# Conditional residual layer on one core: weights of the second category behind two x tiles, bias rows in three loads, first category read from the smallest key

## The chip, the core and the metric

The kernel runs on one core of one Trainium2 chip. The metric is the device time of one execution in microseconds (us). A core has TensorE (PE in the rows; PEld is its weight load), VectorE (DVE), ScalarE (ACT), GpSimd (POOL) and SyncE (SP). SP, ACT and POOL can each put DMA transfers on a queue of their own; all queues are served by the core's 16 DMA engines.

## What is computed

```python
# x: 128 x 128 x 512, ids: 128 values of 0..30, W: 32 x 512 x 512, b: 32 x 512, all f32
selected_W = W[cat_ids]
selected_b = b[cat_ids]
y = jnp.einsum('bti,bio->bto', x, selected_W) + selected_b[:, None, :]
return x + y
```

Each of the 128 batches is a 128 x 512 tile that is multiplied by the 512 x 512 weights of its category; the category's bias row and the tile itself are added. The ids as drawn put 6 batches in category 0, 3 in category 1, 9 in category 2, 4 in category 3 and 1 to 9 in each later one up to 30.

## The kernel before

Batches are worked off sorted by category, so that each category's weights (1 MB) are loaded once. `x` is transposed on the host; tile i of the sorted order is a 256 KB load into `xs` (8 buffers). The identity is added to the weights, so that the product already holds `x` itself. A matmul of f32 precision is put together from rounded parts: ScalarE rounds a tile into its high part `xh` (L268) and copies it to PSUM (`pT`, L271), VectorE subtracts to get the low part `xl` (`low`, L329); GpSimd adds the identity to the raw weights `wr` (L224), rounds them to `wh` (L238) and subtracts to get `wl` (L242). A batch is 12 matmuls (L416): HH (`xh` with `wh`), HL (`xh` with `wl`) and LH (`xl` with `wh`), each over four pieces k of the 512 inputs. VectorE adds the bias row from `bb` to the result (L358) into `os`, and SP stores it (L181). From here on W1, W2, ... are the weights of categories 1, 2, ..., and x3 is tile 3 of the sorted order, batch 3 its matmuls.

The sorted order is found on the chip at the start: VectorE makes a key out of id and position, whose smallest value gives the first tile (`t0`); TensorE, between warm-up matmuls on `fill` (`warm`, L365), transposes and multiplies to make the tables `tb` (which tile), `tc` (category + 1), `tv` (place of the bias row) and `tn` (how many batches are done when a category is). They are raised in this order on `s_tab`. TensorE reads `tc` four entries at a time into registers (`table`) and waits for all four tables ahead of batch 0 (L391).

Category 0 is a special case. Its weights come in two halves on ACT's queue; GpSimd adds the identity piece by piece (L211), ScalarE rounds (L275), VectorE subtracts pieces 1 to 3 (`low_w`, L334) and GpSimd piece 0 (L213). Batch 0 runs its 12 matmuls in the hand-written order `first`.

What each queue carries, in order: SP the ids, x0, x1, x2, x3, W1, x4, x5, x6, and from then on one store and one x load in turn. GpSimd bias row 0; then, when W1 is there and its identity added, W2 and bias rows 1 to 3; when the low part of W1 is written, W3; W4 follows with bias rows 4 to 7, and so on. All instructions of an engine run in the order of the code, and a wait holds everything behind it.

`s_w` tells TensorE how many categories are ready (`wait_ge(s_w, c)`, L397, c being category + 1). For category 1 GpSimd raises it at L248, behind its wait for bias rows 1 to 3 (`s_bb[0]`, L247); for category 2 and later the subtraction L242 raises it.

```python
if c == 1:
    eng.wait_ge(s_wp, 2)
    load(3)
    eng.wait_ge(s_bb[0], 16)
    eng.sem_inc(s_w, 1)
elif c + NR < C:
    eng.wait_ge(s_w, c + 1)
    load(c + NR)
```

Of the kernel before, what the change touches and what calls it, by code (L numbers as in the profile page):

```python
# [5 lines left out]
def cond_resid(nc, xt, ids, W, bias, out):  # L6
# [5 lines left out]
    f32 = mybir.dt.float32  # L12
# [8 lines left out]
    C = 32  # L21
# [13 lines left out]
    with ExitStack() as ctx:  # L35
# [3 lines left out]
        def sem(name):  # L39
            return ctx.enter_context(nc.semaphore(name))  # L40
# [52 lines left out]
        s_oe = sem("s_oe")  # L93
# [3 lines left out]
        s_b0 = sem("s_b0")  # L97
# [21 lines left out]
        def chunk(c, k0, k1):  # L119
            return slice(slot(c) + k0 * D, slot(c) + k1 * D)  # L120
# [30 lines left out]
        @block.sync  # L151
        def _(eng):
            eng.dma_start(idr[:, :], ids.rearrange("(a n) -> a n", a=1)).then_inc(s_id, 16)
            first = eng.alloc_register("first")
            eng.wait_ge(s_t0, 1)
            eng.load(first, t0[0:1, 0:1])
            x_load(eng, 0, bass.ds(eng.snap(first, min_val=0, max_val=B - 1), 1))
            eng.wait_ge(s_tab, 1)
            ahead = table(eng, "la", tb, B, 0, B - 1)
            behind = table(eng, "st", tb, B, 0, B - 1)  # L160
            ahead(0)

            def load(i):
                b = ahead(i)
                if i == NX:
                    eng.wait_ge(s_xl, 2)
                elif i > NX:
                    eng.wait_ge(s_pt, i - NX)
                x_load(eng, i, bass.ds(b, 1))

            for i in range(1, AHEAD):
                load(i)
                if i == 3:
                    eng.dma_start(wr[:, 1, :], W[1, :, :]).then_inc(s_w1, 16)
            for i in range(B):
                if i + AHEAD < B:
                    load(i + AHEAD)
                b = behind(i)
                eng.wait_ge(s_fin, i + 1)
                rows = slice(0, 64 if i == B - 1 else 128)  # L180
                eng.dma_start(out[bass.ds(b, 1), rows, :].rearrange("a t d -> (a t) d"), os[rows, i % NO, :])\  # L181
                   .then_inc(s_o[i % NO], 16)
            for i in range(NO):
                eng.wait_ge(s_o[i], 16 * len(range(i, B, NO)))
            eng.wait_ge(s_oe, 16)

        @block.gpsimd
        def _(eng):
# [19 lines left out]
            for k in range(KT):  # L208
# [3 lines left out]
            eng.wait_ge(s_rh, 1)  # L212
            eng.tensor_tensor(wl[:, chunk(0, 0, 1)], raw(0, 0, 1), wh[:, chunk(0, 0, 1)].bitcast(f32),  # L213
                              ALU.subtract).then_inc(s_wp, 1)
            bias_load(eng, 0, 1, s_b0)

            done = table(eng, "dn", tn, C, 1, B + 1)
            for c in range(1, C):
# [6 lines left out]
                if c == 1:  # L225
                    eng.wait_ge(s_rh, KT)
                    eng.wait_ge(s_wd, 3)
                    eng.wait_ge(s_wp, 1)  # L228
                    load(2)
                    bias_load(eng, 1, NB, s_bb[0])  # L230
# [9 lines left out]
                if c > 1 and c % NB == 0:  # L240
                    eng.wait_ge(s_bb[c // NB], 16)
                eng.tensor_tensor(wl[:, at], wr[:, c % NR, :], wh[:, at].bitcast(f32),  # L242
                                  ALU.subtract).then_inc(s_wp if c == 1 else s_w, 1)
                if c == 1:
                    eng.wait_ge(s_wp, 2)
                    load(3)
                    eng.wait_ge(s_bb[0], 16)  # L247
                    eng.sem_inc(s_w, 1)  # L248
                elif c + NR < C:
                    eng.wait_ge(s_w, c + 1)  # L250
                    load(c + NR)

        @block.scalar
        def _(eng):
# [23 lines left out]
            for i in range(1, B):  # L278
                high(i)
            end = eng.alloc_register("end")  # L280
            eng.wait_ge(s_tab, 1)
            eng.load(end, tb[0:1, B - 1:B])
            b = eng.snap(end, min_val=0, max_val=B - 1)
            eng.wait_ge(s_fin, B)
            eng.dma_start(out[bass.ds(b, 1), 64:128, :].rearrange("a t d -> (a t) d"), os[64:128, (B - 1) % NO, :])\
               .then_inc(s_oe, 16)

        @block.vector
        def _(eng):
# [14 lines left out]
            link(eng.tensor_reduce(low1[:, :], key[:, :], AX.X, ALU.min))  # L304
# [31 lines left out]

            eng.wait_ge(s_bat, 2)
            eng.tensor_scalar(tc[:, :], pA[2][0:1, 0:128], 1.0 / B, 1.0, ALU.mult, ALU.add).then_inc(s_tab, 1)
            eng.wait_ge(s_tab, 2)
# [3 lines left out]
            low(0)  # L343
            for k in range(1, KT):
                low_w(k)
            low(1)
            eng.wait_ge(s_tab, 4)
            row = table(eng, "bo", tv, B, 0, (C - 1) * D)
            for i in range(B):
# [3 lines left out]
                if i == 0:  # L353
                    eng.wait_ge(s_b0, 16)
# [7 lines left out]
        def _(eng):  # L362
            def warm(n):
                for _ in range(n):
# [4 lines left out]
            warm(5)  # L369
# [14 lines left out]
            first = [(HH, 0), (HH, 1), (LH, 0), (LH, 1), (HH, 2), (LH, 2), (HL, 0), (HL, 1),  # L384
                     (HH, 3), (LH, 3), (HL, 2), (HL, 3)]
# [4 lines left out]
            at_reg = eng.alloc_register("at")  # L390
            eng.wait_ge(s_tab, 4)  # L391
            for i in range(B):
                c = row(i)
# [8 lines left out]
                for n, (p, k) in enumerate(first if i == 0 else early if i < 3 else plain):  # L402
                    if i > 0 and (p, k) == (LH, 0):
                        eng.wait_ge(s_xl, i + 2)
# [5 lines left out]
                    if i == 0 and p == HL:  # L410
                        if k == 0:
                            eng.wait_ge(s_wp, 1)
                        else:
                            eng.wait_ge(s_wd, k)
# [28 lines left out]
```

## Time and profile before

| | us |
|---|---|
| median of 3 runs | 367.55 |
| the three runs | 364.81, 367.55, 368.1 |
| the profiled execution | 370.41 |
| its span, first instruction to last | 368.4 |
| TensorE matmuls busy | 358.0 (97%) |
| GpSimd busy | 270.6 (73%) |
| VectorE busy | 172.5 (47%) |
| ScalarE busy | 146.6 (40%) |

All rows come from the profiled execution, and their times count from the start of its span. Busy shares are averages over a start-up of some 40 us and a long even stretch behind it. In rows of the timeline "x4" is four instructions merged into one row, and the bracket gives how long the engine was idle before it and what released it. A matmul's time in a row holds its latency; matmuls overlap, so four of them that take 1.07 follow the next four after 0.91.

### The profile page before, as it was taken

The page shows a single profiled execution, that of the slowest core. Times are in us where ns is not written, and L with a number is a line of the kernel's source. Part 1 is how long each engine was busy: PE and PEld are TensorE (multiplying, and loading weights), DVE is VectorE, ACT ScalarE, POOL GpSimd, SP SyncE. Part 2 cuts the span into 40 slices and gives each one's busy share as a digit, 9 for nine tenths or more (in the row PEclk, how much of TensorE's full clock was granted, in tenths as well). Part 3 has the DMA queues.
Part 4 walks back from the last instruction along what each step waited for, and adds up shares of the span by engine and source line. Part 5 has one row for each costly group of instructions (what it writes and reads, how often), then busy time and mean ns, then how long its engine had stood idle before and what let it go on. Part 6 is the DMA issues. An engine that isn't in the chain of part 4 may idle for free.

```text
span 368.4 us, 7354 instructions
## 1 busy us (share of the span) xinstructions
PE 358.0 (97%) x1553; PEld 291.3 (79%) x1553; DVE 172.5 (47%) x278; ACT 146.6 (40%) x262; POOL 270.6 (73%) x147
## 2 busy tenths in 40 slices
PE   7987999999999999999999999999999999999995
PEld 2766888888888888888888888888888888888884
DVE  6452454454544544445445454454454544545441
ACT  4433334334433434433444344342443343434320
POOL 6187999999285598889992999799988899934000
PEclk9996999999999999999999999999999999999999
DMA  6898899999967898889998699989998999965522
GB/s 199 283 313 318 312 357 336 308 330 406 332 223 284 308 338 308 284 306 362 360 318 302 239 372 329 325 284 372 345 320 300 354 363 296 323 212 187 192 104 87
DMA packets 42904, 109.54 MB, mean 297 GB/s; under 512 B 4785, under 2 KB 4786, under 8 KB 38002
## 3 DMA queue, kind: packets, MB, share of 16 engines
q1 hardware_dynamic: 36946, 68.04, 51.9%
q0 software_dynamic: 5552, 39.85, 31.2%
q10 hardware_dynamic: 368, 1.18, 0.9%
q8 instruction: 19, 0.31, 0.3%
q14 instruction: 19, 0.16, 0.1%
HBM read 75.50 MB, written 33.55 MB: 296 GB/s over the span
## 4 chain that ended last, share of the span: by engine, by line
PE 91%; DMA 4%; issue 2%; POOL 1%; DVE 0%; ACTq 0%; POOLq 0%; DVEq 0%
PE pA L416 91%; DMA bb<-bias 3%; DMA wr<-w 1%; POOL wr L224 0%; POOL wl L213 0%; POOL wr L211 0%; POOL bb L132 0%; DVE os L358 0%; POOL wr L202 0%; ACTq L256 0%; DVEq L358 0%; POOLq L228 0%; POOLq L248 0%
## 5 line engine op out<-in xcount | busy, mean ns | idle before, releaser
L358 DVE TENSOR_TENSOR os<-pA,bb 128x512 f32<-128x512 f32 x128 | 88.6, 692 | 180.8 <-PE pA L416 177.0
L268 ACT ACTIVATE xh<-xs 128x512 fp32r<-128x512 f32 x127 | 80.4, 633 | 203.9 <-PE pA L416 118.5
L242 POOL TENSOR_TENSOR wl<-wr,wh 128x2048 fp32r<-128x2048 f32 x31 | 143.4, 4625 | 2.6
L416 PE MATMUL pA<-wh,xl 128*128 x512 | 138.5, 392 | 4.1 <-POOLq L248 3.7
L416 PE MATMUL pA<-wh,xh 128*128 x512 | 138.2, 391 | 0.5 <-issue 0.4
L416 PE MATMUL pA<-wl,xh 128*128 x512 | 138.0, 391 | 0.0
L416 PEld LDWEIGHTS pA<-wh,xl 128*128 128x128 f32 x512 | 96.6, 189 | 25.1 <-issue 5.0
L416 PEld LDWEIGHTS pA<-wh,xh 128*128 128x128 f32 x512 | 96.6, 189 | 21.9 <-issue 1.7
L416 PEld LDWEIGHTS pA<-wl,xh 128*128 128x128 f32 x512 | 96.7, 189 | 20.4 <-issue 0.3
L329 DVE TENSOR_TENSOR xl<-pT,xh 128x512 fp32r<-128x512 f32 x127 | 86.5, 681 | 8.9 <-ACT pT L271 8.9
L238 POOL TENSOR_SCALAR wh<-wr 128x2048 fp32r<-128x2048 f32 x31 | 59.4, 1917 | 39.1 <-PE pA L416 37.3
L271 ACT ACTIVATE pT<-xs 128x512 f32<-128x512 f32 x127 | 74.1, 584 | 0.0
L224 POOL TENSOR_TENSOR wr<-wr,ident 128x512 f32<-128x512 f32 x31 | 40.4, 1304 | 11.5 <-DMA wr<-w 7.8
L202 POOL DMA_DIRECT2D wr<-w x30 | 17.7, 589 | 8.6 <-POOL wl L242 8.6
L365 PE MATMUL pA<-fill 128*128 128x512 bf16 x11 | 5.2, 624 | 1.6 <-DVE unit L299 1.6
L132 POOL DMA_DIRECT2D bb<-bias x9 | 5.0, 556 | 0.0
L365 PEld LDWEIGHTS pA<-fill 128*128 128x128 bf16 x11 | 1.1, 126 | 3.1 <-issue 2.9
L211 POOL TENSOR_TENSOR wr<-wr,ident 128x128 f32<-128x128 f32 x4 | 1.7, 452 | 2.4 <-DMA wr<-w 2.4
L275 ACT ACTIVATE wh<-wr 128x512 fp32r<-128x512 f32 x4 | 2.3, 619 | 2.1 <-POOL wr L211 2.1
L258 ACT ACT_TABLE_LOAD x1 | 1.3, 1283 | 1.7 <-PEq L436 1.7
L334 DVE TENSOR_TENSOR wl<-wr,wh 128x512 fp32r<-128x512 f32 x3 | 1.9, 678 | 0.0
L324 DVE TENSOR_TENSOR xl<-xs,xh 128x256 fp32r<-128x256 f32 x2 | 1.7, 871 | 0.4 <-ACT xh L263 0.4
(42 smaller groups left out, 11.1 us busy)
## 6 DMA issues: line engine op xcount, KB each, us to landing
xs<-xt SPq DMA_DIRECT2D x128, 256.0 KB, 5.5
out<-os SPq DMA_DIRECT2D x127, 256.0 KB, 5.1
wr<-w POOLq DMA_DIRECT2D x30, 1024.0 KB, 7.7
bb<-bias POOLq DMA_DIRECT2D x7, 1024.0 KB, 9.7
wr<-w ACTq DMA_DIRECT2D x2, 512.0 KB, 4.4
wr<-w SPq DMA_DIRECT2D x1, 1024.0 KB, 8.6
bb<-bias POOLq DMA_DIRECT2D x1, 768.0 KB, 11.0
bb<-bias POOLq DMA_DIRECT2D x1, 256.0 KB, 7.7
```

The costliest lines, as they stand in the source:

```text
L132: eng.dma_start(bb[:, at].rearrange("p (c d) -> p c d", c=j1 - j0), bias[j0:j1, :].rearrange("(a c) d -> a c d", a=1).to_broadcast([128, j ...
L202: eng.dma_start(wr[:, c % NR, :], W[c, :, :]).then_inc(s_wr[c % NR], 16)
L224: eng.tensor_tensor(eye, eye, ident[:, :, :], ALU.add).then_inc(s_ri, 1)
L238: eng.tensor_scalar(wh[:, at], wr[:, c % NR, :], 1.0, 1.0, ALU.mult, ALU.mult).then_inc(s_wh, 1)
L242: eng.tensor_tensor(wl[:, at], wr[:, c % NR, :], wh[:, at].bitcast(f32), ALU.subtract).then_inc(s_wp if c == 1 else s_w, 1)
L268: eng.activation(xh[:, i % NH, :, :], xs[:, i % NX, :, :], ACT.Copy).then_inc(s_xh, 1)
L271: eng.activation(pT[i % NT][:, :, :], xs[:, i % NX, :, :], ACT.Copy).then_inc(s_pt, 1)
L275: eng.activation(wh[:, chunk(0, k, k + 1)], raw(0, k, k + 1), ACT.Copy).then_inc(s_rh, 1)
L329: eng.tensor_tensor(xl[:, i % NH, :, :], pT[i % NT][:, :, :], xh[:, i % NH, :, :].bitcast(f32), ALU.subtract).then_inc(s_xl, 1)
L358: eng.tensor_tensor(os[:, i % NO, :], pA[i % NA][:, :], bb[:, bass.ds(at, D)], ALU.add).then_inc(s_fin, 1)
L365: eng.matmul(pA[0][:, :], fill[:, 0:128], fill[:, :], start=True, stop=True)
L416: mm = eng.matmul(pA[i % NA][:, :], xp[:, i % NH, k, :], wp[:, bass.ds(at + k * D, D)], start=(n == 0), stop=(n == 3 * KT - 1))
```

## The change

- SP loads W1 behind x2 instead of behind x3.
- GpSimd loads bias row 0 without a subtraction ahead of it, then row 1 behind W2 and rows 2 and 3 behind W3. Category 1 waits for row 1 alone; category 2 now waits for rows 2 and 3, and its semaphore is raised by a separate instruction behind the issue of W4 and of bias rows 4 to 7.
- The low part of piece 0 of category 0's weights moves from GpSimd to VectorE; pieces 0 and 1 and the low part of x0 stand ahead of `tc`, pieces 2 and 3 and the low part of x1 ahead of `tv` and `tn`.
- TensorE reads the smallest key itself and takes the first category from it (shifted right by 7, and with 31, plus 1); the wait for `tc` and the register load of the table move into batch 0, behind its sixth matmul. There is one warm-up matmul less ahead of the first table matmuls. The order `first` changes.
- The last tile is stored in one piece by SP, not in two halves by SP and ACT.

The diff, cut to its core:

```diff
@@ sync
             for i in range(1, AHEAD):
                 load(i)
-                if i == 3:
+                if i == 2:
                     eng.dma_start(wr[:, 1, :], W[1, :, :]).then_inc(s_w1, 16)
...
-                rows = slice(0, 64 if i == B - 1 else 128)
-                eng.dma_start(out[bass.ds(b, 1), rows, :]...., os[rows, i % NO, :])\
+                eng.dma_start(out[bass.ds(b, 1), :, :]...., os[:, i % NO, :])\
                    .then_inc(s_o[i % NO], 16)
@@ gpsimd
-            eng.wait_ge(s_rh, 1)
-            eng.tensor_tensor(wl[:, chunk(0, 0, 1)], raw(0, 0, 1), wh[:, chunk(0, 0, 1)].bitcast(f32),
-                              ALU.subtract).then_inc(s_wp, 1)
-            bias_load(eng, 0, 1, s_b0)
+            bias_load(eng, 0, 1, s_b0[0])
...
                 if c == 1:
                     eng.wait_ge(s_rh, KT)
-                    eng.wait_ge(s_wd, 3)
-                    eng.wait_ge(s_wp, 1)
+                    eng.wait_ge(s_wd, KT)
                     load(2)
-                    bias_load(eng, 1, NB, s_bb[0])
+                    bias_load(eng, 1, 2, s_b0[1])
...
                 eng.tensor_tensor(wl[:, at], wr[:, c % NR, :], wh[:, at].bitcast(f32),
-                                  ALU.subtract).then_inc(s_wp if c == 1 else s_w, 1)
+                                  ALU.subtract).then_inc(s_wp if c < 3 else s_w, 1)
                 if c == 1:
+                    eng.wait_ge(s_wp, 1)
+                    load(3)
+                    bias_load(eng, 2, NB, s_bb[0])
+                    eng.wait_ge(s_b0[1], 16)
+                    eng.sem_inc(s_w, 1)
+                elif c == 2:
                     eng.wait_ge(s_wp, 2)
-                    load(3)
+                    load(4)
                     eng.wait_ge(s_bb[0], 16)
                     eng.sem_inc(s_w, 1)
@@ scalar
-            eng.wait_ge(s_fin, B)
-            eng.dma_start(out[bass.ds(b, 1), 64:128, :]...., os[64:128, (B - 1) % NO, :])\
-               .then_inc(s_oe, 16)
@@ vector
+            low_w(0)
+            low_w(1)
+            low(0)
             eng.wait_ge(s_bat, 2)
             eng.tensor_scalar(tc[:, :], ...).then_inc(s_tab, 1)
+            low_w(2)
+            low_w(3)
+            low(1)
             eng.wait_ge(s_tab, 2)
             eng.tensor_scalar(tv[:, :], ...).then_inc(s_tab, 1)
             eng.wait_ge(s_bat, 3)
             eng.tensor_scalar(tn[:, :], ...).then_inc(s_tab, 1)
-            low(0)
-            for k in range(1, KT):
-                low_w(k)
-            low(1)
@@ tensor
-            warm(5)
+            warm(4)
+            eng.wait_ge(s_t0, 1)
+            eng.load(lowest, low1[0:1, 0:1])
+            eng.reg_alu(lowest, lowest, 7, ALU.logical_shift_right)
+            eng.reg_alu(lowest, lowest, C - 1, ALU.bitwise_and)
+            eng.reg_alu(lowest, lowest, 1, ALU.add)
+            c0 = eng.snap(lowest, min_val=1, max_val=C)
...
-            first = [(HH, 0), (HH, 1), (LH, 0), (LH, 1), (HH, 2), (LH, 2), (HL, 0), (HL, 1),
-                     (HH, 3), (LH, 3), (HL, 2), (HL, 3)]
+            first = [(HH, 0), (HH, 1), (HL, 0), (HL, 1), (LH, 0), (LH, 1), (HH, 2), (HH, 3),
+                     (LH, 2), (LH, 3), (HL, 2), (HL, 3)]
...
-            eng.wait_ge(s_tab, 4)
             for i in range(B):
-                c = row(i)
+                c = row(i) if i else c0
...
+                    if i == 0 and n == 6:
+                        eng.wait_ge(s_tab, 2)
+                        row(0)
```

Three places show what stands in a row now. On SP, behind the load of the table `tb`, the x tiles and W1 (`wr<-w`) stood like this:

```order
L148 DMA xs<-xt 128x512
L144 ISA
L148 DMA xs<-xt 128x512
L144 ISA
L148 DMA xs<-xt 128x512
L174 DMA wr<-w 128x2048
L143 TENSOR_LOAD tb
L144 ISA
L148 DMA xs<-xt 128x512
```

and stand like this now (line numbers are those of the changed file):

```order
L147 DMA xs<-xt 128x512
L143 ISA
L147 DMA xs<-xt 128x512
L173 DMA wr<-w 128x2048
L143 ISA
L147 DMA xs<-xt 128x512
L142 TENSOR_LOAD tb
L143 ISA
L147 DMA xs<-xt 128x512
```

W1 has moved ahead of the third of these tiles, x3; nothing else on SP has moved. On GpSimd, from the load of bias row 0 (128x512) through categories 1 and 2, before:

```order
L213 TENSOR_TENSOR wl<-wr,wh 128x512
L132 DMA bb<-bias 128x512
L224 TENSOR_TENSOR wr<-wr,ident 128x4x128
L202 DMA wr<-w 128x2048
L132 DMA bb<-bias 128x1536
L238 TENSOR_SCALAR wh<-wr 128x2048
L242 TENSOR_TENSOR wl<-wr,wh 128x2048
L202 DMA wr<-w 128x2048
L224 TENSOR_TENSOR wr<-wr,ident 128x4x128
```

and now:

```order
L131 DMA bb<-bias 128x512
L218 TENSOR_TENSOR wr<-wr,ident 128x4x128
L199 DMA wr<-w 128x2048
L131 DMA bb<-bias 128x512
L231 TENSOR_SCALAR wh<-wr 128x2048
L235 TENSOR_TENSOR wl<-wr,wh 128x2048
L199 DMA wr<-w 128x2048
L131 DMA bb<-bias 128x1024
L218 TENSOR_TENSOR wr<-wr,ident 128x4x128
```

The subtraction ahead of bias row 0 is gone, the load behind W2 has shrunk from three rows to one, and a load of two rows stands behind W3. On TensorE, from the last warm-up matmuls into batch 0, before:

```order
L365 MATMUL pA<-fill 128x512 x3
L143 TENSOR_LOAD tc
L394 REGISTER_ALU
L395 ISA
L416 ISA
L416 MATMUL pA<-wh,xh 128x512
L416 ISA
L416 MATMUL pA<-wh,xh 128x512
L416 MATMUL pA<-wh,xl 128x512 x2
```

and now:

```order
L359 MATMUL pA<-fill 128x512 x3
L394 REGISTER_ALU
L395 ISA
L416 ISA
L416 MATMUL pA<-wh,xh 128x512
L416 ISA
L416 MATMUL pA<-wh,xh 128x512
L416 REGISTER_ALU
L416 MATMUL pA<-wl,xh 128x512
L416 REGISTER_ALU
L416 MATMUL pA<-wl,xh 128x512
L416 MATMUL pA<-wh,xl 128x512 x2
```

The load of the table `tc` no longer stands ahead of batch 0; it comes behind the last row shown, and two HL matmuls stand ahead of the first LH.

## Rows read from the trace of the kernel before

**Rows 1.** The page's first line.

```profile
span 368.4 us, 7354 instructions
```

**Rows 2.** Chain of waits that ended last: start us, us, what.

```profile
18.39 10.97 DMA bb<-bias
...
29.39 0.03 POOLq L248
...
29.54 334.70 PE pA L416 x1464
...
364.36 0.69 DVE os L358
```

**Rows 3.** Timeline of TensorE: start us, us, instruction, [idle before it, releaser].

```profile
7.87 0.73 PE L416 MATMUL pA<-wh,xh 128*128 x2 [0.43 <-issue]
...
17.41 1.18 PE L416 MATMUL pA<-wh,xl 128*128 x4 [0.43 <-DVE xl L329]
...
29.54 2.07 PE L416 MATMUL pA<-wh,xl 128*128 x4 [3.70 <-POOLq L248]
...
40.39 1.07 PE L416 MATMUL pA<-wh,xl 128*128 x4
```

**Rows 4.** Stretches: length, busy us of each engine, granted clock, DMA share, GB/s.

```profile
11.20:14.00 2.80, 2.77 (x12) 2.31 (x13) 0.69 (x1) 0.99 (x3) 0.00 (x0) 1.00 0.96 271
14.00:16.90 2.90, 2.90 (x14) 2.13 (x12) 1.03 (x2) 0.17 (x1) 0.29 (x1) 1.00 0.90 348
...
28.10:28.40 0.30, 0.00 (x0) 0.00 (x0) 0.00 (x0) 0.00 (x0) 0.00 (x0) 0.56 1.08 417
...
29.60:34.90 5.30, 5.30 (x13) 4.14 (x14) 0.69 (x1) 2.20 (x4) 5.12 (x3) 0.50 0.93 374
...
40.40:360.00 319.60, 319.60 (x1412) 264.64 (x1411) 151.75 (x235) 130.14 (x232) 245.28 (x119) 1.00 0.86 306
```

**Rows 5.** Timeline of GpSimd, same columns as rows 3.

```profile
6.86 1.27 POOL L213 TENSOR_TENSOR wl<-wr,wh 128x512 fp32r<-128x512 f32 x1
...
16.61 1.27 POOL L224 TENSOR_TENSOR wr<-wr,ident 128x512 f32<-128x512 f32 x1 [7.78 <-DMA wr<-w]
...
25.89 0.59 POOL L202 DMA_DIRECT2D wr<-w  x1 [0.30 <-POOL wl L242]
29.55 1.27 POOL L224 TENSOR_TENSOR wr<-wr,ident 128x512 f32<-128x512 f32 x1 [3.07 <-DMA bb<-bias]
...
37.77 0.59 POOL L202 DMA_DIRECT2D wr<-w  x1 [0.30 <-POOL wl L242]
38.36 0.53 POOL L132 DMA_DIRECT2D bb<-bias  x1
```

**Rows 6.** DMA issues (KB each, median us to landing), and landings of eight bias loads.

```profile
bb<-bias POOLq DMA_DIRECT2D x1, 256.0 KB, 7.7
...
DMA to landing us min/median/max: 8.5/10.0/11.2
```

**Rows 7.** Timeline of ScalarE (x3, x4, x8) and of VectorE (x4).

```profile
13.05 0.63 ACT L268 ACTIVATE xh<-xs 128x512 fp32r<-128x512 f32 x1 [1.81 <-DMA xs<-xt]
...
17.18 0.63 ACT L268 ACTIVATE xh<-xs 128x512 fp32r<-128x512 f32 x1 [3.01 <-DMA xs<-xt]
...
29.56 0.63 ACT L268 ACTIVATE xh<-xs 128x512 fp32r<-128x512 f32 x1 [7.64 <-DMA xs<-xt]
...
18.40 0.69 DVE L329 TENSOR_TENSOR xl<-pT,xh 128x512 fp32r<-128x512 f32 x1 [0.64 <-ACT pT L271]
```

**Rows 8.** Line 324, VectorE's low part of x0: min/median/max ns.

```profile
L324 DVE TENSOR_TENSOR xl<-xs,xh x2: 414/871/1328, 7.1 to 8.3; 128x256 fp32r<-128x256 f32 x2
```

**Rows 9.** DMA issues of the last ten microseconds.

```profile
out<-os SPq DMA_DIRECT2D x2, 256.0 KB, 2.3
...
out<-os ACTq DMA_DIRECT2D x1, 128.0 KB, 2.7
```

More of the change, by code:

```diff
@@ L92, in cond_resid @@
         s_o = [sem(f"s_o{i}") for i in range(NO)]
-        s_oe = sem("s_oe")
         s_w0 = [sem(f"s_w0{i}") for i in range(2)]
@@ L96, in cond_resid @@
         s_wr = [sem(f"s_wr{i}") for i in range(NR)]
-        s_b0 = sem("s_b0")
+        s_b0 = [sem(f"s_b0{i}") for i in range(2)]
         s_bb = [sem(f"s_bb{i}") for i in range(C // NB)]
@@ L154, in _ @@
             first = eng.alloc_register("first")
-            eng.wait_ge(s_t0, 1)
+            eng.wait_ge(s_t0, 2)
             eng.load(first, t0[0:1, 0:1])
@@ L179, in _ @@
                 eng.wait_ge(s_fin, i + 1)
-                rows = slice(0, 64 if i == B - 1 else 128)
-                eng.dma_start(out[bass.ds(b, 1), rows, :].rearrange("a t d -> (a t) d"), os[rows, i % NO, :])\
+                eng.dma_start(out[bass.ds(b, 1), :, :].rearrange("a t d -> (a t) d"), os[:, i % NO, :])\
                    .then_inc(s_o[i % NO], 16)
@@ L184, in _ @@
                 eng.wait_ge(s_o[i], 16 * len(range(i, B, NO)))
-            eng.wait_ge(s_oe, 16)
         @block.gpsimd
@@ L279, in _ @@
                 high(i)
[L280 to L283, printed above, removed]
-            eng.wait_ge(s_fin, B)
-            eng.dma_start(out[bass.ds(b, 1), 64:128, :].rearrange("a t d -> (a t) d"), os[64:128, (B - 1) % NO, :])\
-               .then_inc(s_oe, 16)
         @block.vector
@@ L303, in _ @@
                                           op0=ALU.mult, op1=ALU.add))
-            link(eng.tensor_reduce(low1[:, :], key[:, :], AX.X, ALU.min))
+            eng.tensor_reduce(low1[:, :], key[:, :], AX.X, ALU.min).then_inc(s_t0, 1)
+            eng.wait_ge(s_t0, 1)
             eng.tensor_single_scalar(t0[:, :], low1[:, :], B - 1, ALU.bitwise_and).then_inc(s_t0, 1)
@@ L353, in _ @@
                 if i == 0:
-                    eng.wait_ge(s_b0, 16)
+                    eng.wait_ge(s_b0[0], 16)
                 eng.wait_ge(s_mm, i + 2)
@@ L368, in _ @@
             eng.sem_inc(s_mm, 1)
-            warm(5)
+            at_reg = eng.alloc_register("at")
+            lowest = eng.alloc_register("lowest")
+            warm(4)
+            eng.wait_ge(s_t0, 1)
+            eng.load(lowest, low1[0:1, 0:1])
[3 more added lines that the diff above has]
+            c0 = eng.snap(lowest, min_val=1, max_val=C)
             eng.wait_ge(s_one, 3)
@@ L389, in _ @@
             row = table(eng, "wo", tc, B, 1, C)
-            at_reg = eng.alloc_register("at")
-            eng.wait_ge(s_tab, 4)
             for i in range(B):
-                c = row(i)
+                c = row(i) if i else c0
                 eng.reg_alu(at_reg, c, NW - 1, ALU.bitwise_and)
@@ L410, in _ @@
                     if i == 0 and p == HL:
[L411 to L414, printed above, removed]
+                        eng.wait_ge(s_wd, k + 1)
                     xp, wp = pair[p]
```

## The prediction

> **What bounds the kernel now.** I read the span and the chain of waits first, then TensorE's timeline, then the engine that the chain names. The span is 368.4 us [rows 1]. In the chain [rows 2] one piece holds 334.70 of it: TensorE's matmuls from 29.54 to 364.24. The reader should see that they run back to back at the end of it: batch 9 starts at 40.39 [rows 3], and the 119 batches from there to 364.24 take 2.72 us each. Whatever is won there must be matmuls left out, and the change leaves none out. So the time is the start of batch 9, plus a fixed 323.85, plus the tail behind the last matmul. Only what stands before 40.39 and after 364.24 can move.
>
> Before 40.39 three things cost TensorE time [rows 3]. Batch 3 waits 0.43 for its low part. Batch 6, the first of category 1, waits 3.70, from 25.84 to 29.54, for a semaphore that GpSimd raises at L248; the chain shows why GpSimd raises it so late: the 768 KB of bias rows 1 to 3, issued at 18.39, take 10.97 to land [rows 2]. And in that idle time the granted clock falls from 1.00 to 0.50 (from 2.4 to 1.2 GHz) at about 28.1, some 2.3 us after TensorE went idle, and stays there to 34.9 [rows 4]. Batches 6 to 8 therefore take 40.39 - 29.54 = 10.85 instead of 3 x 2.72 = 8.16: the stall costs another 2.69.
>
> **The change part by part.**
>
> *Bias rows as one, one, two.* Category 1 now waits for row 1 alone (256 KB behind the second next weights W2), and rows 2 and 3 go behind W3, where category 2 waits for them. What replaces the bias as the last thing before category 1 is GpSimd's own chain. It starts when W1 lands (its addition of the identity starts at 16.61) and reaches the issue of W3 at 25.89, 9.28 later [rows 5]; that stretch holds one weight issue and one bias issue now as before. Behind it come, new ahead of the semaphore, the issue of W3 and of rows 2 and 3: 0.59 and 0.53 by the same pair at 37.77 and 38.36 [rows 5].
>
> *W1 behind two x tiles.* W1 overtakes x3 on SP's queue, 256 KB less ahead of it. At the 271 to 348 GB/s of the two stretches in which it came in [rows 4] that is 0.75 to 0.97 us; I take 0.85. W1's chain then starts at 15.76, W3 is issued at 25.04, and GpSimd reaches the wait for row 1 at 26.16. Row 1 is issued at 18.39 - 0.85 = 17.54. The nearest size, row 0, took 7.7 [rows 6], which gives 25.2; the nearest place, rows 1 to 3 behind the same W2, took 10.97, which gives 28.5. I take the size, because row 1 leaves a third of the bytes behind W2. Category 1 opens at 26.2.
>
> The price of that is x3. It now stands behind 1 MB. It landed by 13.05 [rows 7]; with the same bytes ahead that W1 had, itself included, it lands at about 16.5, where W1 did (the ends: 13.05, and 17.18 where x4 landed). From x4's landing at 17.18 to the end of its low part at 19.09 are 1.91 us [rows 7], so batch 3 starts at 18.4 instead of 17.41, and batch 6 at 18.4 + 8.16 = 26.6. That is later than 26.2: category 1 no longer stalls TensorE, and the stall has moved to batch 3. There TensorE is idle from the end of batch 2 (16.98 before, perhaps 0.8 earlier now) for 1.4 to 2.2 us.
>
> Here a rule and the rows pull apart. x4, the next on SP's queue, was there 0.65 us after W1 [rows 5, 7], less than its 256 KB need by themselves: the transfers of one queue overlap in part, so overtaking x3 may give W1 less than 0.85, down to nothing. The Trainium skill (DMA: Bandwidth & Descriptors, section "Queues, rings and completion order") says that each DMA engine takes turns between queues and works through one queue's ring in order; by it W1 gains the whole 256 KB and x3 waits for the whole of W1. By the rule the saving is the sum below, and by the full overlap 0.85 less.
>
> *Category 2.* It holds only behind category 1's three batches, so it is late next. GpSimd's work on it started at 29.55, when the bias came, and reached the next issue at 37.77, 8.22 later [rows 5]. Now it starts at 26.2 and gets there at 34.4; the issues of W4 and of four bias rows (1.12) stand ahead of the semaphore, and 0.15 passes from L248 to the matmul [rows 2]: 35.7. Rows 2 and 3, issued at 25.6, must be there by 35.5. Eight bias loads took 8.5 to 11.2 with a median of 10.0 [rows 6], so they land between 34.1 and 36.8; at half of those loads' bytes I take them as in time, and 36.8 as the upper end (batch 9 at 37.0). TensorE itself would be ready at 26.6 + 8.16 = 34.8. Its x tiles are close behind: x8 landed only at 29.56 [rows 7], and 1.91 later its low part is there, 31.5 for a batch 8 at 32.0; up to 0.9 of lateness there goes into the wait for category 2. So batch 9 starts at 35.7 instead of 40.39, with a stall of about 0.9 ahead of it: **4.7 us** gained, of which the 3.70 and the 2.69 are the stock and the 1.0 of batch 3 and the 0.9 of category 2 are given back.
>
> *Category from the smallest key; low parts on VectorE.* These act on batches 0 to 2. TensorE idles 0.43 ahead of its first matmul for the register work [rows 3]; with the category known early most of it goes. The register load that replaces it stands ahead of the matmuls that build the tables, on which x1, x2 and W1 wait; it costs 0 to 0.5 (bounded by that same idle time), and one warm-up matmul less gives about as much back, so I take 0. The wait for the tables is now in the middle of batch 0 and may cost up to a microsecond there. GpSimd's subtraction at 6.86 goes [rows 5]; beside it one half of VectorE's subtraction took 1328 ns and the other 414 [rows 8], so VectorE gets 0.9 back and pays it for the quarter of the weights that it takes over, about 0.7 as in [rows 7]. I cost all of it at nothing, either sign up to 0.8: batch 3 waits for x3 until 18.4 whatever batches 0 to 2 do, up to 1.4 us of lateness. Without that cover each would count in full only as far as 34.8 passes 35.7.
>
> *One last store.* The last addition ends at 365.05 [rows 2]; then two halves of 128 KB go out, ACT's taking 2.7 to land. The two whole tiles of 256 KB before them took 2.3 [rows 9]. So a single store ends the kernel 0.4 earlier (0 to 0.6).
>
> **Sum:** 4.7 + 0.4 = 5.1. The profiled execution took 370.41 (span 368.4 and 2.0 around it), which gives 365.3. It lies 2.9 above the median of the three runs, 367.55; taken from that median, 362.4.
>
> **The rivals.**
> *The batch 3 stall lowers the clock* (2 in 10). For: 1.4 to 2.2 us of idle time is near the 2.3 after which it fell [rows 3, 4]. Against: the idle 0.43 at batch 3 did not lower it, and 2.2 is the upper end. It would cost what it cost before, 2.69: batch 9 at 34.8 + 2.7 = 37.5, which hides category 2's stall. 367.55 - 2.9 - 0.4: 364.2.
> *The small bias loads take as long as the large one* (17 in 100). For: row 0 with 256 KB took 7.7, hardly less than far larger ones [rows 6]. Row 1 at 28.5 delays GpSimd's whole chain by 2.3, batch 9 starts at 38.0: 364.8. If only rows 2 and 3 are late, at 36.8, batch 9 starts at 37.0: 363.8.
> *W1 is not earlier* (1 in 10): the part does not do what it says, all GpSimd times slip by 0.85: 363.3.
> *Slower than before* (5 in 100). One mechanism: rows 2 and 3, now queued behind W3's 1 MB, hold category 2 so long that the clock falls in that stall, for another 2.7. It decides from batch 9 at 40.39 + 0.4 - 2.7 = 38.1, so from a landing after 37.9, 12.3 us from the issue. The longest bias load in the trace took 11.2 [rows 6], which speaks against it. A landing at 42 would give about 371.7.
> *More than the sum* (3 in 100): GpSimd is in time, batch 9 at 34.8: 361.5.
>
> **How the numbers follow.** My forecast, that GpSimd's chain sets batch 9 at about 35.7, has 45 in 100, with a range of its own of 361.5 to 363.3. About 1% (3.7 us, 363.9) is what a measurement of this kernel can tell from no change. Below it lie the forecast (0.45), W1 not earlier (0.10), more than the sum (0.03) and about 0.05 of the second rival: 0.63 faster. The rest of the second rival and the clock at batch 3 stay within 1%: 0.32. Slower: 0.05. The range of 361.0 to 366.0 takes in all but the ends of the late bias loads and the slower case, and some spread of the runs, which differ by 3.3 among themselves.
>
> **What would show it.** Right: TensorE's long wait is at batch 3, for the low part of x3, at 18 to 18.8; none over 0.3 at batch 6; about 1 us at batch 9, behind GpSimd's semaphore at about 35.6; W1's identity addition near 15.8; the granted clock at 1.00 from batch 0 on. Wrong: a wait for a bias row that ends after 27 or 36; a granted clock of 0.50 anywhere after 8 us; x3's activation before 15; a tail after the last addition that is not shorter than 3.3; or any wait of TensorE behind 41.

## The result

The changed kernel took 366.31 us (median of 18 runs, 363.13 to 367.09), the kernel before on the same chip 369.94 (18 runs, 364.81 to 371.60). The ratio is 0.9924, with a 95% interval of 0.9895 to 0.9953. It leaves out runs that lie over 1.5% above the fastest of their kernel, so it is nearer one than the ratio of the medians. The change makes the kernel faster by 0.8%: the direction was right, the size was not. Three repeats, below, gave 0.9959, 0.9909 and 0.9971, the last with an interval that reaches one. 362.4 was forecast; 366.31 lies 0.31 above the range, and the gain stays just within the 1%.

The profiled execution tells another story: 370.41 before, 365.86 after, with 365.3 forecast from the first. So the profile bears out most of the mechanism, and the median does not bear out the time. That the profiled run was one at full clock is chance: in 31 of 54 runs of this kernel the clock fell (below). The rows of after come first, then the runs that settle this.

The page's first line, and the end of the chain of waits (start us, us, what), which answer to [rows 1, 2]:

```profile
span 363.7 us, 7350 instructions
25.95 10.19 DMA bb<-bias
36.14 0.02 issue
36.16 0.03 POOLq L247
36.19 0.13 issue
36.31 323.97 PE pA L416 x1428
```

The long piece now starts with batch 9, not with batch 6, and what comes last ahead of it is the new load of bias rows 2 and 3, issued at 25.95. The two stretches of idle time that are left on TensorE are seen in its timeline, which answers to [rows 3] (start us, us, instruction, [idle before it, releaser]); the rows are batch 3, batch 6 and batch 9:

```profile
18.82 1.20 PE L416 MATMUL pA<-wh,xl 128*128 x4 [2.39 <-DVE xl L321]
27.14 1.07 PE L416 MATMUL pA<-wh,xl 128*128 x4
36.31 1.18 PE L416 MATMUL pA<-wh,xl 128*128 x4 [0.86 <-POOLq L247]
```

Batch 6 no longer waits. The long wait is at batch 3, for x3's low part, and there is a shorter one at batch 9. The clock stays at 1.00 from batch 3 to the end (stretches: length, busy us of PE, PEld, DVE, ACT and POOL, granted clock, DMA share, GB/s; compare [rows 4]):

```profile
18.90:22.30 3.40, 3.40 (x15) 2.82 (x16) 2.37 (x5) 2.35 (x5) 3.32 (x2) 1.00 0.92 260
22.40:36.00 13.60, 13.06 (x58) 10.49 (x56) 6.54 (x11) 4.06 (x9) 12.75 (x8) 1.00 1.02 361
36.40:360.00 323.60, 323.60 (x1428) 267.87 (x1428) 151.60 (x235) 130.94 (x234) 246.56 (x120) 1.00 0.86 305
```

GpSimd's chain, answering to [rows 5], with x3's activation on ScalarE (last row) for [rows 7]:

```profile
16.08 1.26 POOL L218 TENSOR_TENSOR wr<-wr,ident 128x512 f32<-128x512 f32 x1 [7.53 <-DMA wr<-w]
25.36 0.59 POOL L199 DMA_DIRECT2D wr<-w  x1 [0.30 <-POOL wl L235]
25.95 0.53 POOL L131 DMA_DIRECT2D bb<-bias  x1
26.50 1.30 POOL L218 TENSOR_TENSOR wr<-wr,ident 128x512 f32<-128x512 f32 x1
36.31 1.29 POOL L218 TENSOR_TENSOR wr<-wr,ident 128x512 f32<-128x512 f32 x1 [0.38 <-DMA bb<-bias]
```
```profile
16.66 0.63 ACT L267 ACTIVATE xh<-xs 128x512 fp32r<-128x512 f32 x1 [5.35 <-DMA xs<-xt]
```

Category 2's work begins at 26.50, where it began at 29.55 before, without a wait for row 1. The tail: the last addition (0.69 long) starts at 360.40 and ends at 361.09, 2.62 before the end of the span; before these were 365.05 and 3.36.

In the profiled executions batch 9 starts 40.39 - 36.31 = 4.08 earlier, the tail is 0.75 shorter, and the stretch of matmuls is 0.12 longer (323.97 against 323.85): 4.7, the difference of the spans.

### The profile page after: what moved, and what is told of

Same layout as the page of the kernel before. It is cut to its first block, busy times and chain, and to the rows that moved or that the text cites. A ratio compares the mean times of both kernels' runs of the same rounds, so it can differ in the third digit from the quotient of the medians.

```text
span 363.7 us, 7350 instructions
## 1 busy us (share of the span) xinstructions
PE 354.8 (98%) x1552; PEld 289.6 (80%) x1552; DVE 172.3 (47%) x279; ACT 146.8 (40%) x262; POOL 270.9 (74%) x147
## 4 chain that ended last, share of the span: by engine, by line
PE 89%; DMA 4%; POOL 3%; issue 2%; DVE 0%; ACTq 0%; DVEq 0%; POOLq 0%
PE pA L416 89%; DMA bb<-bias 3%; DMA wr<-w 1%; POOL wl L235 1%; POOL wh L231 1%; POOL wr L208 1%; POOL wr L218 0%; POOL bb L131 0%; POOL wr L199 0%; DVE os L352 0%; ACTq L255 0%; DVEq L352 0%; POOLq L247 0%; POOLq L221 0%
## 5 line engine op out<-in xcount | busy, mean ns | idle before, releaser
L208 POOL TENSOR_TENSOR wr<-wr,ident 128x128 f32<-128x128 f32 x4 | 2.7, 695 | 2.4 <-DMA wr<-w 2.4
L326 DVE TENSOR_TENSOR wl<-wr,wh 128x512 fp32r<-128x512 f32 x4 | 2.8, 745 | 0.0
```

Source lines behind the costliest of these rows:

```text
L208: eng.tensor_tensor(eye, eye, ident[:, 0:1, :], ALU.add).then_inc(s_ri, 1)
```

## The experiments

The theory (C in the expectations): the stall that the change moves to batch 3 is long enough that the granted clock falls behind it in a part of the runs, though not in the profiled one; and the kernel before also mixes runs with and without a fall. Rivals: the landing of bias rows 2 and 3 varies from run to run (D); the start of the program or W1's order costs something that the prediction set to nothing; the bias split gains nothing; W1 would gain nothing by moving further ahead (E).

**The changed kernel again**, without an edit.

> The changed kernel once more, beside its variants on one chip. In its profiled execution the granted clock stayed at 1.00 and batch 9 started at 36.31 us, 4.1 before the old 40.39, so by that execution the gain is 4.7; its runs gave less, and ten of them report a mean granted clock of 0.994 or 0.995, eight 0.998 or more. Theory C (the clock falls in the 2.39 us wait ahead of batch 3 in some executions): about half of the runs with a mean clock near 0.995, those 1 to 2 us slower than the others; a profile that catches one shows a clock of 0.50 just behind 18 us. Theory D (the landing of bias rows 2 and 3 varies): no tie between clock and time; in the profile the wait ahead of batch 9 differs from 0.86 by as much as the span differs from 363.7.

366.56 (364.95 to 367.95, 12 runs) beside 368.83 for before (35 runs); ratio 0.9959 (0.9922 to 0.9997). This time the profiled run shows the fall. TensorE's timeline at batch 3, and stretches behind it (columns as above):

```profile
19.05 1.25 PE L416 MATMUL pA<-wh,xl 128*128 x4 [2.18 <-DVE xl L321]
20.10 1.91 PE L416 MATMUL pA<-wl,xh 128*128 x4
```
```profile
19.10:20.00 0.90, 0.90 (x4) 0.78 (x5) 0.90 (x3) 0.90 (x2) 0.90 (x1) 1.00 0.93 230
20.10:23.40 3.30, 3.30 (x9) 2.62 (x8) 1.10 (x2) 1.03 (x2) 3.22 (x2) 0.50 0.99 268
23.50:36.00 12.50, 12.50 (x57) 10.34 (x56) 6.44 (x10) 4.49 (x8) 11.71 (x8) 1.00 1.02 378
```

The engine stood idle 2.18, restarted at 19.05 at 1.00, and about a microsecond later ran at 0.50 (1.2 GHz) until some 23.4. Batch 3 took 4.45 until batch 4, not 2.88, and batch 9 started at 37.11 without a wait, 0.8 later than in the run above: the wait for category 2 had absorbed the rest. Bias rows 2 and 3 were in time here, and the span was longer all the same, so D does not explain it.

Each run also lists its mean clock, and the kernel's runs fall into groups by it. Over 54 runs of the changed kernel and 104 of before, each from four series on several chips:

| mean clock of the run | before: runs, median us | changed: runs, median us |
|---|---|---|
| 0.997 and over | 28, 366.31 | 23, 364.95 |
| 0.992 to 0.996 | 41, 369.11 | 28, 366.53 |
| 0.991 and less | 35, 370.82 | 3, 368.42 |

The profiled runs named here with 0.991 to 0.995 all show a stretch at 0.50 in or behind their long wait, and the changed kernel's with 0.998 or more show none. So by its mean the clock fell in 31 of 54 runs of the changed kernel, and in 76 of 104 of before. The profiled run of before, with 0.991, belongs to its last group, 4.51 above its first. The plain means are 368.86 and 365.97, so the change gains 2.9 over all runs and 1.36 between the groups at full clock (0.3 to 2.1 by resampling; the chips are not the same in both). The sorting doesn't say what a fall costs by itself: runs in which it falls may also have the longer stall. The runs with matmuls in the stall, below, tell the two apart.

**Warm matmuls ahead of batch 3.** Eight matmuls on constants stand in the stall; batch 3 overwrites their result.

```diff
             for i in range(B):
+                if i == 3:
+                    for _ in range(8):
+                        eng.matmul(pA[3][:, :], fill[:, 0:128], fill[:, :], start=True, stop=True)
                 c = row(i) if i else c0
```

> Eight extra matmuls on the warm-up tile, into a PSUM buffer that batch 3 overwrites, stand ahead of batch 3's waits, so TensorE works for about 1.7 of the 2.4 us in which it waits for x3. Nothing else changes. Theory C: the clock cannot fall there, all runs report a mean clock of 0.998 or more, and the median falls by 1 to 1.7 us against the changed kernel on the same chip. Theory D: mean clocks and median as in the changed kernel, within 0.5 us.

365.60 (363.88 to 366.44, 12 runs), 0.96 below the changed kernel on the same chip (95% by resampling: 0.17 to 1.77); the mean clock was 0.998 or more in all 12 runs, where it was so in 4 of 12. Nothing else was altered, so the stall at batch 3 is shown to be what lowers the clock, and 0.96 is what comes back in the median when it is filled. The matmuls can cost time of their own: in the profile the low part of x3 was there at 17.42, and batch 3 started behind them at 17.91.

```profile
16.37 1.90 PE L395 MATMUL pA<-fill 128*128 128x512 bf16 x8
17.91 1.28 PE L419 MATMUL pA<-wh,xl 128*128 x4
```

This profile, with a span of 361.7 the shortest of the 12, held something else: W1 came 3 us earlier than in the profile of after (GpSimd's addition of the identity to W1):

```profile
13.18 1.27 POOL L218 TENSOR_TENSOR wr<-wr,ident 128x512 f32<-128x512 f32 x1 [4.54 <-DMA wr<-w]
```

The warm matmuls, at 16.37, can't have done that. The last section comes back to it.

**W1 behind x3 again** (one part undone).

```diff
-                if i == 2:
+                if i == 3:
                     eng.dma_start(wr[:, 1, :], W[1, :, :]).then_inc(s_w1, 16)
```

> Undoes one part: W1 stands behind x3 again. By my prediction's theory (GpSimd's chain and the bias rows behind it set batch 9): W1 lands about 0.5 us later (16.5), batch 3 starts near 16.7 with next to no wait, category 1 opens near 26.6 and batch 6 waits 1.8 us for it, category 2 opens at 36.6 to 36.8, so batch 9 starts 0.3 to 0.5 later than in the changed kernel. Rival (the wait for x3 is what the change pays): batch 9 starts 1 to 2 us earlier than in the changed kernel.

367.44 (10 runs), 0.89 above the changed kernel (-0.13 to 1.86: not settled); the clock fell in 6 of 10. The stall is back at batch 6 (first row); what GpSimd waits for last ahead of it, 0.45, is bias row 1, which took 8.91 to land here. In front of batch 9 there is a shorter one:

```profile
26.96 1.19 PE L416 MATMUL pA<-wh,xl 128*128 x4 [1.63 <-POOLq L242]
35.83 1.19 PE L416 MATMUL pA<-wh,xl 128*128 x4 [0.43 <-POOLq L247]
```

In this profile W1's addition starts at 16.08, just as in that of after: the order as such did not bring W1 in earlier there.

**Bias rows 1 to 3 in one load again** (one part undone; W1 stays behind x2).

```diff
-                    bias_load(eng, 1, 2, s_b0[1])
+                    bias_load(eng, 1, NB, s_bb[0])
...
-                    bias_load(eng, 2, NB, s_bb[0])
-                    eng.wait_ge(s_b0[1], 16)
-                    eng.sem_inc(s_w, 1)
-                elif c == 2:
-                    eng.wait_ge(s_wp, 2)
-                    load(4)
                     eng.wait_ge(s_bb[0], 16)
```

> Undoes one part: bias rows 1 to 3 come in one load behind W2 again, and category 1 waits for all of them; all else as changed. By my theory they land 11 us after their issue at 17.9, at 28.9, so batch 6 starts at 29.0 with a wait of about 1.9 us, GpSimd starts category 2 there, and batch 9 waits until about 37.1, or 37.2 by its own matmuls: 0.9 us later than in the changed kernel, and more where the clock falls in the wait at batch 6. Rival (the split of the bias rows is most of the gain): batch 9 at 39.5 or later.

366.19 (10 runs), no difference from the changed kernel (-0.37, from -1.81 to 0.62). GpSimd does wait for the large load, 2.09 until 28.44:

```profile
28.44 1.28 POOL L218 TENSOR_TENSOR wr<-wr,ident 128x512 f32<-128x512 f32 x1 [2.09 <-DMA bb<-bias]
```

but TensorE waited 2.85 at batch 3 and then ran at 0.50 until about 24, so that batch 6 came only at 29.14, behind the bias. The stall at batch 3 covers it.

**Both undone**: the two edits above together; the early category, the low parts and the one store stay.

> W1 behind x3 again and bias rows 1 to 3 in one load behind W2, so both edits to GpSimd's chain are undone together; the early category, the low parts, the order of batch 0 and the single last store stay as changed. If the two edits cover for each other (each alone moves the stall out of batch 6 far enough), undoing both brings the old stall back: batch 6 waits 2.5 to 4 for a bias semaphore that comes near 28.5 to 29.5, the clock falls to 0.50 in or behind that wait in most runs (mean clock 0.988 to 0.995), batch 9 starts at 39 to 40.5, and the median stands 0 to 1.2 below the kernel before on the same chip, the 0.75 of the single store within that, and 2 or more above the changed kernel. If the gain comes from the start of the program or the store instead, the median stays within 0.7 of the changed kernel and batch 9 starts before 38.

368.69 (365.75 to 371.27, 12 runs), and the changed kernel on the same chip, as

> The changed kernel, as the reference on the same chip: median 365.6 to 366.8, 1 to 4 below the kernel before. In a part of the runs, about half, the mean clock is 0.991 to 0.995 and the time 366.4 to 368.5; in the others 0.998 or more and 363 to 366.4. Its profile shows TensorE's only long wait behind batch 0 at batch 3, for the low part of x3, 1.2 to 2.4.

366.30 (12 runs; ratio to before 0.9971, 0.9932 to 1.0009). Both undone is 2.39 slower than that (1.47 to 3.18), and not distinguishable from before (ratio 1.0030, 0.9989 to 1.0071). The old stall is back, with the clock behind it (batch 6, then two stretches):

```profile
28.54 2.07 PE L410 MATMUL pA<-wh,xl 128*128 x4 [2.72 <-POOLq L241]
```
```profile
28.60:31.50 2.90, 2.90 (x7) 2.32 (x8) 0.69 (x1) 1.72 (x4) 2.81 (x2) 0.50 1.08 429
31.70:38.00 6.30, 6.30 (x29) 5.21 (x28) 2.58 (x4) 2.24 (x4) 5.90 (x5) 1.00 0.81 300
```

So the gain hangs on the order of W1 and the bias split together, 2.4 of it; singly undone they cost 0.9 (not settled) and nothing that can be measured; in the two profiles above either alone moves or shortens the old stall. The rest, 0.4 by the medians (368.69 against 369.11), is what store and early start have left, and it is not distinguishable from nothing; the store alone shortens the tail by 0.75 in the trace.

**Warm matmuls in the kernel before**, ahead of its stall at batch 6.

```diff
             for i in range(B):
+                if i == 6:
+                    eng.wait_ge(s_fin, i - NA + 1)
+                    for _ in range(14):
+                        eng.matmul(pA[i % NA][:, :], fill[:, 0:128], fill[:, :], start=True, stop=True)
                 c = row(i)
```

> The kernel before, with one thing added: fourteen matmuls on the warm-up tile ahead of batch 6, into a PSUM buffer that batch 6 overwrites, so that TensorE works for about 3 of the 3.7 us in which it waits for bias rows 1 to 3. It takes no wait away. Theory C (a good part of the old stall's price, and of its spread from run to run, is the clock): mean clocks of 0.998 or more in all runs and a median 2 to 2.5 us under the old kernel's, that is, nearly the whole gain of the change without any of its edits. Rival (the gain is the shorter wait for the bias): a median within 0.7 us of the old kernel's.

367.94 (366.42 to 369.47, 12 runs) beside 369.15: 1.2 less (0.3 to 2.1 by resampling), where 2 to 2.5 were expected, and a ratio that can't be told from one (0.9990, 0.9959 to 1.0022). The mean clock was 0.997 or more in 10 of 12. In its profile the matmuls (one of the 14 has no record) fill the wait, the clock stays at 1.00, and batches 6 to 8 take 37.01 - 28.72 = 8.29, where they took 10.85 (the rows: the matmuls, batch 6, batch 9):

```profile
25.67 2.97 PE L396 MATMUL pA<-fill 128*128 128x512 bf16 x13
28.72 1.18 PE L420 MATMUL pA<-wh,xl 128*128 x4
37.01 1.09 PE L420 MATMUL pA<-wh,xl 128*128 x4
```

So even with the clock kept up the kernel before takes 367.9, not the 366.31 of its own runs at full clock. Either the groups of the table differ by the stall as well as by the clock, or the matmuls, which end at 28.64, hold up batch 6 in runs where the bias comes earlier; nothing here tells the two apart. Against the medians of before beside them, this kernel stands at 0.9967 (367.94 / 369.15), and the changed one with warm matmuls at 0.9912 (365.60 / 368.83). With the falls taken from both, 0.55%, about 2.0 us, of the gain is left (0.4 to 3.4 by resampling); by the ratios 0.9990 and 0.9962 it is 0.28%, 1.0. The two profiles without a fall, 365.1 here and 363.7 of after, differ by 1.4. So an estimated 1 to 2 us of the gain come from the shorter stalls and the tail and the rest from the clock; the division is not settled.

**The late start**: category, low parts and the order of batch 0 as before; W1, bias and store as changed.

```diff
-            low_w(0)
-            low_w(1)
-            low(0)
             eng.wait_ge(s_bat, 2)
             eng.tensor_scalar(tc[:, :], ...).then_inc(s_tab, 1)
...
-                c = row(i) if i else c0
+                c = row(i)
```

> Keeps the second weights behind two x tiles, the bias rows in three loads and the single last store, and undoes the rest: TensorE again takes the first category from the table and waits for all tables, with five warm-up matmuls, the old order in batch 0, and the low part of piece 0 on GpSimd. My prediction's working: batches 0 to 2 end about 0.6 us later and batch 3 starts when x3's low part is there, as in the changed kernel, so batch 9 moves by less than 0.3. Theory C adds: the wait ahead of batch 3 shrinks from 2.4 to about 1.8, so the clock falls in fewer runs and the median is 0 to 0.8 us under that of the changed kernel. Rival (the early start is a gain): 0.5 us or more slower than the changed kernel.

365.79 (12 runs), ratio to before 0.9929 (0.9894 to 0.9964), where the whole change has 0.9924 (0.9895 to 0.9953): these edits are worth nothing that these intervals could show, either way. In the profile batch 0 starts at 7.79, 0.60 later than in after; batch 3 waits for x3 in this kernel too (2.38, until 19.24), as the prediction had it.

**W1 on ScalarE's queue**, behind W0, instead of SP's.

```diff
                 eng.dma_start(raw(0, 2 * n, 2 * n + 2), W[0, ...]).then_inc(s_w0[n], 16)
+            eng.dma_start(wr[:, 1, :], W[1, :, :]).then_inc(s_w1, 16)
```

> One edit to the changed kernel: W1 goes onto ACT's queue right behind the two halves of W0, where the DMA engines have nothing to do between 6 and 7.5 us, and is gone from SP's queue. If GpSimd's chain, which starts when W1 lands, and the loads behind it set the start-up, then W1 lands at 9.5 to 11, x3 near 11, batch 3 starts without a wait at about 16.4, category 1 opens near 21 and category 2 near 31, ahead of TensorE at 24.6 and 32.8, and batch 9 starts at 32.5 to 33.5 instead of 36.31: 3 to 4 us less, and no idle time in which the clock can fall, so 4 to 5 us under the changed kernel's median. Rival (the DMA engines' bandwidth sets the start-up, whoever goes first): x1 and x2 come late, batches 1 to 3 wait, x8 comes after 28, and the gain is under 1.5 us.

366.35 (12 runs), ratio 0.9956 (0.9923 to 0.9988). W1 came at 9.2, but x0, on the other queue, 3.0 later than in after (its activation started at 9.57, not at 6.58):

```profile
9.57 0.42 ACT L261 ACTIVATE xh<-xs 128x256 fp32r<-128x256 f32 x1 [3.02 <-DMA xs<-xt]
10.19 1.22 PE L415 MATMUL pA<-wh,xh 128*128 x2 [2.65 <-issue]
```

Batch 0 started at 10.19 instead of 7.19, no batch waited behind it, and batch 9 started at 36.22, against 36.31 in after. What the stalls gave back, the start took.

**W1 further ahead on SP's queue**, all on one chip: the changed kernel as reference, W1 behind x1, and W1 right behind x0.

```diff
-                if i == 2:
+                if i == 1:
                     eng.dma_start(wr[:, 1, :], W[1, :, :]).then_inc(s_w1, 16)
```
```diff
             x_load(eng, 0, bass.ds(eng.snap(first, min_val=0, max_val=B - 1), 1))
+            eng.dma_start(wr[:, 1, :], W[1, :, :]).then_inc(s_w1, 16)
             eng.wait_ge(s_tab, 1)
...
-                if i == 2:
-                    eng.dma_start(wr[:, 1, :], W[1, :, :]).then_inc(s_w1, 16)
```

> The changed kernel as the reference for the two others on one chip: a median of 366 to 367 us, in half of the runs a mean clock near 0.995, and those about 1.2 us slower than the rest.

> W1 moves one more place forward on SP's queue, behind x1. Theory E (W1's megabyte holds up every tile that is issued behind it, and what is held up is needed sooner the further forward W1 goes): W1 lands 0.3 to 0.9 us earlier (15.2 to 15.8), x2 and x3 land around 16, so TensorE waits ahead of batch 2, from 13.5 to about 17.5, and the clock falls in most runs; batch 9 starts no more than 0.5 earlier than 36.31 and the median is 0 to 1 us over the changed kernel's. Rival (each place that W1 gains is time gained): 0.5 us or more under the changed kernel.

> W1 is issued by SP right behind x0, before the tables are known, at about 4.1 us, so that it comes in while the DMA engines had nothing to do between 6 and 7.5 us. On ACT's queue it landed at 9.1 and cost x0 3.0 us, and nothing stalled behind that; behind x0 on one queue it cannot pass x0. Theory E: x0 lands by 6.8, W1 at 9.5 to 10.5, x1 at 10.5 to 11.5, so batch 1 starts 0.3 to 1.3 later than 10.83, no later batch waits, batch 9 starts at 33.2 to 34.5, the mean clock is 0.998 or more, and the median is 2 to 3 us under the changed kernel. Rival (bandwidth is the limit, whoever goes first): x8 comes after 31 and batch 8 or 9 waits, the gain is under 1 us.

The changed kernel took 365.77 (12 runs, ratio 0.9909); behind x1 362.85 (362.51 to 364.04, 6 runs), ratio 0.9836 (0.9785 to 0.9888); behind x0 362.55 (362.48 to 363.54, 6 runs), ratio 0.9836 (0.9784 to 0.9888). Both beat both kernels: 2.9 and 3.2 below the changed one (0.8 to 3.8, and 1.0 to 4.0), and in all 12 runs the clock is 0.998 or more. That W1 would gain nothing further ahead has fallen. Behind x0, W1's addition, x1's activation, and batches 1, 6 and 9:

```profile
9.50 1.52 POOL L217 TENSOR_TENSOR wr<-wr,ident 128x512 f32<-128x512 f32 x1 [0.95 <-DMA wr<-w]
```
```profile
10.10 0.63 ACT L266 ACTIVATE xh<-xs 128x512 fp32r<-128x512 f32 x1 [1.58 <-DMA xs<-xt]
```
```profile
10.98 1.19 PE L415 MATMUL pA<-wh,xh 128*128 x4
24.97 1.07 PE L415 MATMUL pA<-wh,xl 128*128 x4
33.13 1.07 PE L415 MATMUL pA<-wh,xl 128*128 x4
```

With W1 ahead of all x tiles but the first, TensorE waits nowhere behind batch 0: batch 9 starts at 33.13, 3.2 earlier than in after. Behind x1 one stall is left at batch 2, in the profile of the slowest of its six runs; in none of the six did the clock fall:

```profile
15.34 1.20 PE L416 MATMUL pA<-wh,xh 128*128 x4 [1.65 <-ACT xh L267]
```

## Why the prediction was wrong, by its own steps

**The base** is the step that failed first and carried the time out of the range: the prediction took a gain worked out for one run off the median of others. The sum of 5.1 was made from the profiled run (370.41) and then taken off a median of three, 367.55. But it contained what that profiled run paid, the 3.70 of the stall and the 2.69 of the clock. By the table above a run at 367.55 will not have paid all of it (the clocks of those three runs are not on record), so the full sum could not come off it. The median of 18 is 369.94. From the profiled run the same sum gives 365.3, against 365.86 for the profiled run after. The prediction saw the difference of 2.9 and didn't ask what it consisted of; the three runs (364.81, 367.55, 368.10), next to a profile that shows the clock falling, said that the stock to be won varies from run to run.

**The chance of the rival "the batch 3 stall lowers the clock"** was the second. It was given 2 in 10 and came in 31 of 54 runs. Its argument that "2.2 is the upper end" failed: the waits at batch 3 were 2.39, 2.18 and 2.61 in three profiles of the changed kernel, and 1.20 in the fourth. In two of these four the clock fell to 0.50, which it had named as a sign of being wrong. The fourth and the third:

```profile
18.10 1.19 PE L416 MATMUL pA<-wh,xl 128*128 x4 [1.20 <-DVE xl L321]
19.13 2.07 PE L416 MATMUL pA<-wh,xl 128*128 x4 [2.61 <-DVE xl L321]
```

The fall in the trace of before came 2.3 into an idle time, and so the prediction looked only for a fall inside the wait; in one of the two it came a microsecond behind it. The price of 2.69 holds for the old stall (10.85 - 8.29 = 2.56 by the profile with warm matmuls), but for the new one it was too high: 0.96 in the median, by the run with warm matmuls. In the first trace that shows the fall, 0.50 held for some 3.3, against from about 28.1 to 34.9 before, and the wait for category 2 took up part of it.

The miss of 3.91 adds up from these: 369.94 - 367.55 = 2.39 from the base, 0.96 from the clock, and 5.1 - 4.7 = 0.4 from the terms below, 3.75 together. The first two are differences of medians, the last is one of profiles, so that they fit this closely is in part luck.

**Sizes of terms.**
- *4.7 for the start of batch 9* is 40.39 - 35.7; the parts that the prediction gives for it (3.70 and 2.69, less 1.0 and 0.9) add up to 4.5 only.
- *W1 0.85 earlier*: 0.53 (16.61 to 16.08), the same as with the order undone. The prediction's doubt, that overtaking x3 may give less "down to nothing", is what these two profiles show; in two others with the changed order W1 came over 2 us earlier, far more than 0.85, and the last section has why that is no measure of the overtaking.
- *Batch 3 at 18.4*: 18.82. x3 landed at 16.66, for which 16.5 was said.
- *Category 1 without a stall, batch 6 at 26.6*: right, 27.14 without a wait. That GpSimd's chain would be ready first was right too.
- *Rows 2 and 3 in time by 35.5*: no. They took 10.19, about the median (10.0) of the eight loads of [rows 6], and landed at 36.14. Half the bytes brought them no sooner. The prediction named the interval and chose its favourable part; a bias wait that ends after 36 was one of its signs of being wrong. Batch 9 came at 36.31, not 35.7: 4.08 instead of 4.7. The landing made only about 0.2 of that: GpSimd itself was through with its issues at 35.94, not 35.54, mostly because W1 had come 0.32 later than reckoned. In the profiles of again and again3 it did not wait for these rows.
- *One last store 0.4*: 0.75. The whole tile's tail is 2.62, the halves' 3.36; the landing times of [rows 9], 2.7 and 2.3, held only half of the difference, and where the other half sits was not tried.
- *Category and low parts at nothing*: not contradicted, by the late start. Batch 0 has 0.28 in its middle, at the load of `tc`.

**The rivals.** That small bias loads take as long as large ones held for rows 2 and 3 (its 36.8 for the landing), but not for row 1, for which the changed kernel waited in none of its four profiles. The slower case did not come: it needed a landing after 37.9. The rule of the Trainium skill on queue order that the prediction cites (DMA: Bandwidth & Descriptors, section "Queues, rings and completion order") is borne out where it is plainest: with W1 right behind x0, x0 kept its place (activation at 6.60, against 6.58 in after) and x1 came 0.60 after W1; with W1 on another queue, where the rule has the DMA engines take turns, x0 lost 3.0. For an overtaking by one tile the traces show nothing either way: with the same order W1's landing varies by up to 3.2 from run to run, and the saving would be 0.85.

## What to carry to other kernels

A sum made from one profiled run must be taken off that run; if the median differs, ask which terms the typical run doesn't have, first among them a fall of the clock, which made a stall dearer here and didn't come in every run. A stall that is moved is judged by its new length against the shortest one behind which the clock fell (2.18 here), looking behind its end too. And where a large load must overtake small ones, try every place in the queue: two places further ahead was worth another 3.2 here, about as much as the whole change.

## What the runs showed of the hardware

**A fall that comes after the restart.** The clock fell at about 20.1 although TensorE had been back at work since 19.05 at 1.00 (rows of the changed kernel again). A wait of 2.18 was followed by a fall, one of 2.39 by none, one of 2.38 (the late start) by a fall again, and in the third profile of the changed kernel that waits over 2 (2.61) it fell inside the wait: the length of the wait alone does not decide in these runs. Waits of 1.20 here and of 1.63 (W1 behind x3) and 1.65 (behind x1) were followed by none in the profiles. Work without use in the gap kept the clock up in 12 of 12 runs at batch 3, and in 10 of 12 at batch 6 of the kernel before.

**The same load lands at two times.** W1, behind the same tiles, was ready at 13.18 and 13.77 in two profiles (spans 361.7, 361.8) and at 16.08 to 16.39 in three (spans 363.7 to 364.4). Such a load reports 16 landings. In the first two all 16 came between 12.3 and 13.7; in the later ones the first came as early (12.2 to 12.6), but three, seven and eleven of the 16 came only after 15, the last at 16.0 to 16.3. Why, stays open; it goes with about 2 us of the span.

**Two engines that slow each other, seen from the other side.** With VectorE's subtractions moved beside them, two identity additions of GpSimd took 1.84 in all, where they took 0.87 before:

```profile
4.83 0.87 POOL L208 TENSOR_TENSOR wr<-wr,ident 128x128 f32<-128x128 f32 x2 [2.09 <-DMA wr<-w]
6.01 1.84 POOL L208 TENSOR_TENSOR wr<-wr,ident 128x128 f32<-128x128 f32 x2 [0.31 <-DMA wr<-w]
```

Both rows are of the changed kernel; beside the first VectorE did small work, beside the second its subtraction of the weights' first two pieces. In the late start, where the subtractions are back in their old place, the second pair took 0.87 again. It is the counterpart of [rows 8]; no long wait for it shows in the trace.
